# A hand-pipelined cross-attention and mixture kernel: the numerator a quarter later and ahead of kv on TensorE, delta and normalisation last in VectorE's quarter

## The chip, the core and the metric

The kernel runs on one core of a Trainium2 chip. The metric is the device time of one execution in microseconds. Before the change the median of three executions is 493.07 us (491.03 to 505.27). Float32 is used throughout, but for an exponential whose result is thrown away and for two operands of one product that are held as a high and a low part.

## What is computed

The input `x` has 8 x 512 rows of 2048 numbers, and so has the context. One attention layer and one mixture of low-rank experts (four experts, the best two of each row), each on a layer-normalised `x` and each added to `x`:

```python
def _L0_xattn_ref(q, k, v):              # q: layernorm(x); k = v: the context
    qh = q.transpose(0, 2, 1).reshape(B, N, H, dh)     # N = 2048, dh = 32
    ...
    qh = jax.nn.softmax(qh, axis=3)
    kh = jax.nn.softmax(kh, axis=1)
    kvs = jnp.einsum('bnhd,bnhe->bhde', kh, vh)
    out = jnp.einsum('bnhd,bhde->bnhe', qh, kvs)

def _L0_ffn_ref(x, router_w, A, B):      # x: layernorm(x + attention)
    logits = flat @ router_w.T
    topk_vals, topk_idx = jax.lax.top_k(logits, TOP_K)
    ...
    gates = jax.nn.softmax(sparse, axis=-1)
    mid = jnp.einsum('tf,erf->ter', flat, A)
    all_deltas = jnp.einsum('ter,eor->teo', mid, B) * LORA_SCALE
    delta = jnp.einsum('te,teo->to', gates, all_deltas)

x = x + _L0_xattn_ref(_layernorm(x), ctx, ctx)
x = x + _L0_ffn_ref(_layernorm(x), router_w, A, B)
```

(With 512 rows and 8 heads a head is 64 rows, so a tile of 128 rows holds two heads.)

## The kernel before, in words

The 4096 rows are 32 tiles of 128 rows, and each tile is cut into four groups of 512 columns. Nothing schedules the kernel but its text: every engine runs one loop over a step number `q` from -8 to 153, and in each step it does one group of each stage that is due. A step is called a quarter here. `tile_at(q, offset)` gives the tile `t` and the group `g` of a stage in quarter `q`: the stage does group `g` of tile `t` in quarter 4t + g + offset. Stages that come once in a tile ask for g = 0. The second layer works on pairs of tiles, with `pair_at` and `delta_at`. So a pair takes eight quarters, and within them the quarters are named here by q modulo 8 (0 to 7). Engines run ahead of each other as far as the semaphores let them.

The stages, with the engine, the name of the function, the line of the profile and the offset before the change:

- VectorE: `max_part` (L566, -8) the column maximum of the context; `bn_part` (L582, -4) the statistics of `x`, `ln1` (L589, L591) their end; `max_whole` (L575), once a tile, the maximum over the partitions of a turned tile; `kv_recip` (L611, offset 3), once a tile; `normalise` (offset 4) a reciprocal `rden` (L619) of the denominators in `num_ps` and the product `attnT` (L622); `add_delta` (L631) adds `delta_ps` to `y_sb`, which is the output; and, once a pair, a dozen small instructions of the router (`gate_...`), most of them in quarter 2; `mid_low` (L722) once a pair.
- TensorE: `delta` (L431, L432) makes `delta_ps`; `turn_max` and `spread_kmax` (L326, L333) once a tile; `kv` (L348, offset 0) 8 chunks of the product of keys and values; `project` (L384, offset 6) the router's and the experts' projection of `y_sb`; `fold_squares` (L398) once a tile, 32 matmuls, in quarters 2 and 6; `numerator` (L367, offset 4) makes `num_ps`; `turn_mid` (L417) once a pair. This is also their order in a quarter.
- GpSimd (POOL): `shift` (L275, -3) the context minus its maximum into `ek_sb`; `add_x` (L287, offset 4) adds `attnT` to `y_sb`; `root1` and `root2` (L295, L302 to L307).
- ScalarE (ACT): `keys` (L471) the exponential of `ek_sb` by half tiles, `queries` (L478) that of `x_sb`, in place, `square_x1` (L489) the squares of `y_sb`, and small copies (`spread_row` L464, `copy_kv` L499, `copy_squares` L507, `mid_high` L526).
- SyncE (SP): one queue that issues all transfers: `load_ctx` (L216), `load_x` (L220), `load_y` (L223) and `store` (L230), 1 MB each, each behind its wait.

There is one buffer each for `num_ps` and `delta_ps`: `numerator` of a group waits until `normalise` of the one before has read the bank (`attn_made`), and `delta` waits for the `add_delta` before it (`out_made`). `x_sb` has four tiles, and `load_x` of tile t waits for the last numerator of tile t - 4.

Of the kernel before, what the change touches and what calls it, by code (L numbers as in the profile page):

```python
# [44 lines left out]
def xattn_lora_moe_kernel(nc, x, xt, ctxt, wt, bt, consts, out):  # L45
# [11 lines left out]
    with ExitStack() as stack:  # L57
# [156 lines left out]
        def _(sp):  # L214
# [31 lines left out]
            for q in range(0, LAST + 3):  # L246
                p, i = delta_at(q - 1)
                if p is not None and i in (3, 7):
                    store(p, i // 4, 1 if p < NP - 1 else 4)
                t, g = tile_at(q, -12)  # L250
                if t is not None and t >= 4 and g == 0:
                    sp.wait_ge(kv_done, 4 * (t - 4) + 4)
                    load_ctx(t)
                t, g = tile_at(q, -8)
                if t is not None and t >= 3 and g == 0:
                    after(sp, num_done, 4 * (t - 4) + 4)
                    load_x(t)
                t, g = tile_at(q, -1)
                if t is not None and t >= 2 and g == 0:
                    if t >= 8:  # L260
                        old = (t - 8) // 2
                        sp.wait_ge(out_stored[old % 4], 32 * (old // 4 + 1))
                    load_y(t)
# [4 lines left out]
        def _(pool):  # L268
# [43 lines left out]
            for q in range(FIRST, LAST + 1):  # L312
                shift(*tile_at(q, -3))
                root2(q)
                add_x(*tile_at(q, 4))
                root1(q)

        @block.tensor
        def _(pe):
# [124 lines left out]
            for q in range(FIRST, LAST + 1):  # L444
# [4 lines left out]
                if q == 1:  # L449
                    sum_w()  # L450
                kv(*tile_at(q, 0))
                project(*tile_at(q, 6))
                fold_squares(q)
                numerator(*tile_at(q, 4))
# [3 lines left out]
        def _(act):  # L458
# [73 lines left out]
            for q in range(FIRST, LAST + 1):  # L532
                T, r = divmod(q, 4)
                if r == 0:
                    mid_high(q)
                    copy_kv(T - 1)
                    square_x1(T - 2, 1)
                    queries(T - 1, 1)
                if r == 1:
                    spread_row(T + 1)  # L540
                    keys(T, 1)
                if r == 2:
                    gate_exp(q)
                    square_x1(T - 1, 0)
                if r == 3:
                    copy_squares(T - 2)
                    keys(T + 1, 0)
                    queries(T, 0)
# [9 lines left out]
        def _(dve):  # L558
# [43 lines left out]
            def kv_recip(q):  # L602
                t, g = tile_at(q, 3)
# [121 lines left out]
            for q in range(FIRST, LAST + 1):  # L725
# [4 lines left out]
                mid_low(q)  # L730
# [4 lines left out]
                max_part(*tile_at(q, -8))  # L735
                if a is not None:
                    gate_centre(a)
                if b is not None:
                    gate_beats(b, 1)
                    gate_mask(b)  # L740
                ln1(q)
                add_delta(*delta_at(q))
                bn_part(*tile_at(q, -4))
# [4 lines left out]
                if not early:  # L748
                    max_whole(q)
                kv_recip(q)  # L750
                normalise(*tile_at(q, 4))
# [66 lines left out]
```

## Time and profile before

| | |
|---|---|
| median of three executions | 493.07 us (491.03 to 505.27) |
| the profiled execution | 493.56 us, of which its span (first to last instruction) 491.8 us |
| TensorE busy | 404.7 us (82%) |
| VectorE busy | 416.6 us (85%) |
| GpSimd busy | 358.9 us (73%) |
| ScalarE busy | 241.4 us (49%) |
| mean granted clock of TensorE | 0.944 |
| moved by DMA | 137.95 MB, mean 281 GB/s |

A timeline row gives the start and the length of an instruction (or of a run of alike ones) in us, and in brackets how long its engine had been idle before it and what ended that. Instructions of one engine overlap a little: on VectorE rows of 0.68 us start 0.60 us apart. A row of waits adds up such idle times by who waited for whom.

### The profile page before, as it was taken

Reading aid. Unit: us, or ns where it says so; the run is one execution under the profiler, and the core shown is the slowest. Engines: PE = TensorE matmul, PEld = TensorE weight load, DVE = VectorE, ACT = ScalarE, POOL = GpSimd, SP = SyncE. Lnnn points to the kernel's source line nnn. Section 1 sums busy time; section 2 is a strip of 40 time slices with the busy share of each in tenths; the row PEclk is TensorE's granted clock in tenths of the full one; section 3 lists DMA queues with packets and bytes.
Section 4 is the critical chain, followed back from the end, with each engine's and each line's share of the span. In section 5 each row is a group of like instructions: output and inputs, shape, how many; then the busy total and the mean of one; then the engine's idle time right before and its main releaser. Section 6 shows DMA issues by size and latency. Waiting matters only on the chain.

```text
span 491.8 us, 22601 instructions
## 1 busy us (share of the span) xinstructions
PE 404.7 (82%) x9960; PEld 346.6 (70%) x9960; DVE 416.6 (85%) x1109; ACT 241.4 (49%) x340; POOL 358.9 (73%) x341
## 2 busy tenths in 40 slices
PE   5477877979988898879888898979889887989764
PEld 5466766868777677768776777868677676878543
DVE  2598888989998999899987999989999998976652
ACT  1155556545555455555555356545655556564100
POOL 1369997878888787878877787887878786985200
PEclk9568999999999998999998999999999999999955
DMA  8987686587979797787977698887879795532243
GB/s 332 427 329 291 253 315 259 205 311 285 345 263 344 273 390 255 263 332 297 379 279 296 260 331 336 286 316 274 320 282 367 267 384 213 195 152 91 112 188 128
DMA packets 24689, 137.95 MB, mean 281 GB/s; under 512 B 2192, under 2 KB 4368, under 8 KB 12176
## 3 DMA queue, kind: packets, MB, share of 16 engines
q1 hardware_dynamic: 24592, 136.51, 73.5%
q8 instruction: 78, 1.28, 1.0%
q14 instruction: 19, 0.16, 0.1%
HBM read 102.95 MB, written 33.55 MB: 278 GB/s over the span
## 4 chain that ended last, share of the span: by engine, by line
PE 39%; DVE 35%; issue 16%; DMA 4%; POOL 3%; ACT 2%; SPq 1%; DVEq 0%; POOLq 0%
DVE y_sb L631 9%; PE num_ps L367 8%; DVE max_n L566 8%; PE kv_ps L348 7%; PE kv_ps L398 6%; PE delta_ps L431 6%; PE raw_ps L384 6%; DVE bn_parts L582 4%; DMA sq_a<-in_bt_dram 4%; PE delta_ps L432 3%; DVE rden L619 3%; DVE attnT L622 3%; POOL y_sb L287 2%; DVE rz L611 1%; DVE midT L722 1%
## 5 line engine op out<-in xcount | busy, mean ns | idle before, releaser
L287 POOL TENSOR_TENSOR y_sb<-attnT,y_sb 128x512 f32<-128x512 f32 x128 | 164.6, 1286 | 78.6 <-DVE attnT L622 77.3
L275 POOL TENSOR_TENSOR ek_sb<-ctx_sb,kmax_row 128x512 f32<-128x512 f32 x128 | 167.5, 1311 | 15.7 <-ACT kmax_row L464 15.7
L431 PE MATMUL delta_ps<-midT,b_hi 128*128 128x256 f32 x256 | 83.3, 346 | 38.2 <-DVE y_sb L631 37.0
L367 PE MATMUL num_ps<-kv_sb,x_sb 64*64 64x65 f32 x4096 | 94.5, 228 | 8.6 <-issue 7.5
L631 DVE TENSOR_TENSOR y_sb<-delta_ps,y_sb 128x512 f32<-128x512 f32 x128 | 87.5, 683 | 15.8 <-PE delta_ps L432 15.3
L348 PE MATMUL kv_ps<-ctx_sb,ek_sb 128*64 128x65 f32 x2048 | 94.0, 234 | 7.0 <-issue 4.2
L566 DVE TENSOR_REDUCE max_n<-ctx_sb 128x32 f32<-128x512 f32 x128 | 86.4, 677 | 10.8 <-DMA ctx_sb<-in_ctxt_dram 10.4
L622 DVE TENSOR_TENSOR attnT<-num_ps,rden 128x512 f32<-128x512 f32 x128 | 88.5, 691 | 4.6 <-DVE rden L619 0.2
L348 PEld LDWEIGHTS kv_ps<-ctx_sb,ek_sb 128*64 128x64 f32 x2048 | 75.1, 140 | 22.9 <-issue 8.8
L367 PEld LDWEIGHTS num_ps<-kv_sb,x_sb 64*64 64x64 f32 x4096 | 75.2, 137 | 22.6 <-issue 15.0
L384 PE MATMUL raw_ps<-w_sb,y_sb 128*64 128x69 f32 x2048 | 86.6, 225 | 4.4 <-issue 4.4
L431 PEld LDWEIGHTS delta_ps<-midT,b_hi 128*128 128x128 f32 x256 | 50.7, 198 | 54.7 <-DVE y_sb L631 30.3
L582 DVE BATCH_NORM_STATS2 bn_parts<-x_sb 128x6 f32<-128x512 f32 x128 | 87.5, 683 | 0.0
L478 ACT ACTIVATE x_sb<-x_sb,nbias,rstd 128x1024 f32<-128x1024 f32 x64 | 78.6, 1227 | 0.0
L384 PEld LDWEIGHTS raw_ps<-w_sb,y_sb 128*64 128x64 f32 x2048 | 74.5, 137 | 5.5 <-issue 5.1
L432 PE MATMUL delta_ps<-midT,b_lo 128*128 128x256 f32 x256 | 69.8, 293 | 2.3 <-issue 2.3
L471 ACT ACTIVATE ek_sb<-ek_sb 128x1024 f32<-128x1024 f32 x64 | 67.3, 1052 | 4.6 <-POOL ek_sb L275 3.6
L489 ACT ACTIVATE sq_a<-y_sb 128x1024 f32<-128x1024 f32 x32 | 33.9, 1059 | 69.9 <-POOL y_sb L287 69.9
L489 ACT ACTIVATE sq_b<-y_sb 128x1024 f32<-128x1024 f32 x32 | 33.9, 1058 | 61.7 <-POOL y_sb L287 61.7
L432 PEld LDWEIGHTS delta_ps<-midT,b_lo 128*128 128x128 f32 x256 | 51.8, 202 | 0.0
L619 DVE RECIPROCAL rden<-num_ps 128x8 f32<-128x8 f32 x128 | 25.9, 202 | 29.2 <-PE num_ps L367 28.2
L517 ACT ACTIVATE gexp<-below_max,rstd 128x4 f32<-128x4 f32 x32 | 7.8, 289 | 46.5 <-POOL rstd L307 41.9
(55 smaller groups left out, 324.7 us busy)
## 6 DMA issues: line engine op xcount, KB each, us to landing
ctx_sb<-in_ctxt_dram SPq DMA_DIRECT2D x32, 1040.0 KB, 5.6
x_sb<-in_x_dram SPq DMA_DIRECT2D x32, 1024.0 KB, 8.0
y_sb<-in_xt_dram SPq DMA_DIRECT2D x32, 1024.0 KB, 9.7
out_dram<-y_sb SPq DMA_DIRECT2D x30, 1024.0 KB, 5.9
out_dram<-y_sb SPq DMA_DIRECT2D x8, 256.0 KB, 2.1
sq_a<-in_bt_dram SPq DMA_DIRECT2D x1, 1024.0 KB, 18.5
w_sb<-in_wt_dram SPq DMA_DIRECT2D x1, 552.0 KB, 10.8
cst<-in_consts_dram SPq DMA_DIRECT2D x1, 145.0 KB, 2.3
```

The costliest lines, as they stand in the source:

```text
L275: pool.tensor_tensor(ek_sb[:, t % 2, chunks(g), :].rearrange("p (a b) c -> p a b c", b=2), ctx_sb[:, t % 4, 2 * g:2 * g + 2, 1:P + 1, :].r ...
L287: pool.tensor_tensor(y, attnT[:, g, :], y, ALU.add).then_inc(x1_made, 1)
L348: mm = pe.matmul(kv_ps[t % 2][d, h:h + DH + 1], ek_sb[:, t % 2, j, d], ctx_sb[:, t % 4, j // 2, v, j % 2], start=(j == 0), stop=(j == NCH ...
L367: mm = pe.matmul(num_ps[n, h, j * (DH + 1):(j + 1) * (DH + 1)], x_sb[d, t % 4, c * P + half * DH:c * P + (half + 1) * DH], kv_sb[d, t % 2, ...
L384: mm = pe.matmul(raw_ps[p % 2][c, odd, 0:NQ], y_sb[:, t % 8, j, c], w_sb[:, j, :], start=(odd == 0 and j == 0), stop=(j == NCH - 1), skip_ ...
L431: pe.matmul(to, b_hi[:, j * P:(j + 1) * P], midT[:, p % 2, :], start=True, stop=False)
L432: mm = pe.matmul(to, b_lo[:, j * P:(j + 1) * P], midT[:, p % 2, :], start=False, stop=True)
L478: act.activation(half, half, ACT.Exp, bias=nbias1[:, t % 4:t % 4 + 1], scale=rstd1[:, t % 4:t % 4 + 1]).then_inc(q_made, 1)
L566: dve.tensor_reduce(max_n[:, t % 2, c], ctx_sb[:, t % 4, :, 1 + g * 32:33 + g * 32, :].rearrange("p a c b -> p c a b"), AX.XY, ALU.max).th ...
L582: dve.bn_stats(bn_parts[:, t % 4, g, :], x_sb[:, t % 4, cols(g)]).then_inc(bn_parts_made, 1)
L622: dve.tensor_tensor(attnT[:, g, :].rearrange("p (k b d) -> p b k d", b=2, d=DH), heads[:, :, :, 0:DH], rden[:].unsqueeze(3).to_broadcast([ ...
L631: dve.tensor_tensor(y, delta_ps[:].rearrange("p (j t c) -> p t j c", j=2, t=2), y, ALU.add).then_inc(out_made, 1)
```

## The change

The numerator moves from offset 4 to offset 5 and, within TensorE's quarter, from behind `project` and `fold_squares` to the place ahead of `kv`. What follows it moves a quarter with it: `normalise` and `add_x` to offset 5, `project` to offset 7. `kv_recip` goes from offset 3 to 4 and to the second place in VectorE's quarter; `bn_part`, `ln1` and `max_whole` come ahead of `mid_low` and `add_delta`, so that `add_delta` and `normalise` are the last large instructions of a VectorE quarter. On ScalarE both `square_x1` halves come later (the first in the next tile's quarter 0, the second behind `keys` in quarter 1), and `queries(T, 0)` goes from quarter 3 to quarter 2. On SyncE `load_x` moves by one quarter. Nothing is added or removed: each engine runs the same instructions with the same operands.

```diff
@@ sync
-                t, g = tile_at(q, -8)
+                t, g = tile_at(q, -7)
                 if t is not None and t >= 3 and g == 0:
                     after(sp, num_done, 4 * (t - 4) + 4)
                     load_x(t)
@@ gpsimd
-                add_x(*tile_at(q, 4))
+                add_x(*tile_at(q, 5))
@@ tensor
+                numerator(*tile_at(q, 5))
                 kv(*tile_at(q, 0))
-                project(*tile_at(q, 6))
+                project(*tile_at(q, 7))
                 fold_squares(q)
-                numerator(*tile_at(q, 4))
                 turn_mid(q)
@@ scalar
                 if r == 0:
                     mid_high(q)
+                    square_x1(T - 2, 0)
                     copy_kv(T - 1)
-                    square_x1(T - 2, 1)
                     queries(T - 1, 1)
                 if r == 1:
                     spread_row(T + 1)
                     keys(T, 1)
+                    square_x1(T - 2, 1)
                 if r == 2:
                     gate_exp(q)
-                    square_x1(T - 1, 0)
+                    queries(T, 0)
                 if r == 3:
                     copy_squares(T - 2)
                     keys(T + 1, 0)
-                    queries(T, 0)
@@ vector, kv_recip
-                t, g = tile_at(q, 3)
+                t, g = tile_at(q, 4)
@@ vector, the loop
-                mid_low(q)
                 if b is not None:
                     gate_beats(b, 0)
                 if c is not None:
                     gate_mid(c)
                 max_part(*tile_at(q, -8))
+                kv_recip(q)
                 if a is not None:
                     gate_centre(a)
                 if b is not None:
                     gate_beats(b, 1)
                     gate_mask(b)
+                bn_part(*tile_at(q, -4))
                 ln1(q)
+                if not early:
+                    max_whole(q)
+                mid_low(q)
                 add_delta(*delta_at(q))
-                bn_part(*tile_at(q, -4))
                 if a is not None:
                     gate_logits(a)
                 if b is not None:
                     gate_rank(b)
-                if not early:
-                    max_whole(q)
-                kv_recip(q)
-                normalise(*tile_at(q, 4))
+                normalise(*tile_at(q, 5))
```

On TensorE, in the middle of the program, quarters 1 and 2 of a pair stood like this before (`delta_ps` is the mixture's product, `kv_ps` the attention's, `raw_ps` the projection, `num_ps` the numerator):

```order
L431 MATMUL delta_ps<-midT,b_hi 128x256
L432 MATMUL delta_ps<-midT,b_lo 128x256
L333 MATMUL turn_ps<-cst,kmax 128x128
L348 MATMUL kv_ps1<-ctx_sb,ek_sb 64x65 x8
L384 MATMUL raw_ps1<-w_sb,y_sb 64x69 x8
L367 MATMUL num_ps<-kv_sb,x_sb 64x65 x16
L431 MATMUL delta_ps<-midT,b_hi 128x256
L432 MATMUL delta_ps<-midT,b_lo 128x256
```

and stand like this now:

```order
L431 MATMUL delta_ps<-midT,b_hi 128x256
L432 MATMUL delta_ps<-midT,b_lo 128x256
L333 MATMUL turn_ps<-cst,kmax 128x128
L367 MATMUL num_ps<-kv_sb,x_sb 64x65 x16
L348 MATMUL kv_ps1<-ctx_sb,ek_sb 64x65 x8
L384 MATMUL raw_ps1<-w_sb,y_sb 64x69 x8
L431 MATMUL delta_ps<-midT,b_hi 128x256
L432 MATMUL delta_ps<-midT,b_lo 128x256
```

The numerator has gone from the end of the quarter to the place behind the delta.

On VectorE, quarters 3 and 4 of a pair stood like this before (`rz` is `kv_recip`, `midT` is `mid_low`):

```order
L566 TENSOR_REDUCE max_n<-ctx_sb 128x32
L631 TENSOR_TENSOR y_sb<-delta_ps,y_sb 128x2x256
L582 BN_STATS bn_parts<-x_sb 128x6
L611 RECIPROCAL rz<-kv_ps0 64x1 x2
L619 RECIPROCAL rden<-num_ps 128x8
L622 TENSOR_TENSOR attnT<-num_ps,rden 128x2x4x64
L722 TENSOR_TENSOR midT<-raw_ps1,midT 64x256
L566 TENSOR_REDUCE max_n<-ctx_sb 128x32
L589 BN_AGGR bn_out<-bn_parts 128x2
L591 TENSOR_SCALAR var1e<-bn_out 128x1
L631 TENSOR_TENSOR y_sb<-delta_ps,y_sb 128x2x256
L582 BN_STATS bn_parts<-x_sb 128x6
```

and stand like this now, but for the first two:

```order
L631 TENSOR_TENSOR y_sb<-delta_ps,y_sb 128x2x256
L619 RECIPROCAL rden<-num_ps 128x8
L622 TENSOR_TENSOR attnT<-num_ps,rden 128x2x4x64
L566 TENSOR_REDUCE max_n<-ctx_sb 128x32
L611 RECIPROCAL rz<-kv_ps0 64x1 x2
L582 BN_STATS bn_parts<-x_sb 128x6
L589 BN_AGGR bn_out<-bn_parts 128x2
L591 TENSOR_SCALAR var1e<-bn_out 128x1
L575 TENSOR_REDUCE kmax<-turn_ps 128x1
L722 TENSOR_TENSOR midT<-raw_ps1,midT 64x256
L631 TENSOR_TENSOR y_sb<-delta_ps,y_sb 128x2x256
L619 RECIPROCAL rden<-num_ps 128x8
```

Between the start of a quarter and `add_delta` there is now `bn_stats` too, and `rz` and the other small work of the tile have moved ahead of both readers of TensorE's results.

On the SyncE queue a tile's four transfers now stand like this (before, `x_sb` stood ahead of `out_dram`):

```order
L216 DMA ctx_sb<-in_ctxt_dram 128x2080
L230 DMA out_dram<-y_sb 128x2x1024
L220 DMA x_sb<-in_x_dram 128x2048
L223 DMA y_sb<-in_xt_dram 128x2048
```

The load of `x` is now behind a store that waits for `add_delta` of quarter 4 or 0.

## Rows read from the trace of the kernel before

**Rows 1.** Windows of four stretches: busy us by engine, granted clock, DMA share, GB/s.

```profile
core 0: us, PE busy (x) PEld busy (x) DVE busy (x) ACT busy (x) POOL busy (x), PEclk, DMA share, GB/s
34.00:84.00 50.00, 39.10 (x1128) 33.47 (x1130) 41.49 (x110) 28.00 (x38) 44.26 (x39) 0.93 0.74 283
84.00:425.00 341.00, 295.02 (x7699) 253.32 (x7702) 316.21 (x850) 183.50 (x260) 275.77 (x260) 0.99 0.80 299
425.00:458.00 33.00, 30.62 (x829) 26.35 (x824) 26.01 (x82) 17.87 (x26) 24.18 (x25) 1.00 0.35 130
458.00:492.00 34.00, 19.80 (x133) 15.06 (x132) 14.85 (x35) 2.21 (x5) 2.37 (x4) 0.64 0.42 155
```

**Rows 2.** Waits, 84 to 425 us: total us, times, longest.

```profile
POOL y_sb L287 <- DVE attnT L622: 61.9, 61, 2.7
...
PE delta_ps L431 <- DVE y_sb L631: 26.9, 30, 1.5
...
DVE rden L619 <- PE num_ps L367: 15.2, 23, 3.2
```

**Rows 3.** Waits, 34 to 84 us.

```profile
DVE rden L619 <- PE num_ps L367: 7.2, 7, 2.0
...
PE kv_ps L348 <- ACT ek_sb L471: 2.6, 3, 0.9
```

**Rows 4.** Timeline of VectorE, one quarter 6 (columns as told above).

```profile
364.30 0.68 DVE L566 TENSOR_REDUCE max_n<-ctx_sb 128x32 f32<-128x512 f32 x1
364.89 0.68 DVE L631 TENSOR_TENSOR y_sb<-delta_ps,y_sb 128x512 f32<-128x512 f32 x1
365.49 0.69 DVE L582 BATCH_NORM_STATS2 bn_parts<-x_sb 128x6 f32<-128x512 f32 x1
366.45 0.21 DVE L619 RECIPROCAL rden<-num_ps 128x8 f32<-128x8 f32 x1 [0.28 <-PE num_ps L367]
366.70 0.69 DVE L622 TENSOR_TENSOR attnT<-num_ps,rden 128x512 f32<-128x512 f32 x1
```

**Rows 5.** Timeline of TensorE, the same quarter 6, with the delta ahead of it.

```profile
362.88 0.39 PE L431 MATMUL delta_ps<-midT,b_hi 128*128 128x256 f32 x1
...
363.55 0.71 PE L348 MATMUL kv_ps<-ctx_sb,ek_sb 128*64 128x65 f32 x16
364.10 0.66 PE L384 MATMUL raw_ps<-w_sb,y_sb 128*64 128x69 f32 x16
364.68 0.65 PE L398 MATMUL kv_ps<-sq_a,cst 128*32 128x128 f32 x16
...
365.69 0.70 PE L367 MATMUL num_ps<-kv_sb,x_sb 64*64 64x65 f32 x32
```

**Rows 6.** Timeline of TensorE, a gap with no releaser, and near the end.

```profile
265.85 0.94 PE L384 MATMUL raw_ps<-w_sb,y_sb 128*64 128x69 f32 x13 [1.89 <-issue]
...
462.49 0.39 PE L431 MATMUL delta_ps<-midT,b_hi 128*128 128x256 f32 x1
```

**Rows 7.** Timeline of VectorE behind that gap, and the last normalise.

```profile
269.73 0.21 DVE L619 RECIPROCAL rden<-num_ps 128x8 f32<-128x8 f32 x1 [3.15 <-PE num_ps L367]
...
457.29 0.69 DVE L622 TENSOR_TENSOR attnT<-num_ps,rden 128x512 f32<-128x512 f32 x1
```

**Rows 8.** Timeline of ScalarE in the first stretch.

```profile
68.97 1.06 ACT L489 ACTIVATE sq_b<-y_sb 128x1024 f32<-128x1024 f32 x1 [2.07 <-POOL y_sb L287]
...
71.22 1.04 ACT L471 ACTIVATE ek_sb<-ek_sb 128x1024 f32<-128x1024 f32 x1
```

**Rows 9.** Timeline of GpSimd, the first two add_x.

```profile
35.78 2.19 POOL L287 TENSOR_TENSOR y_sb<-attnT,y_sb 128x512 f32<-128x512 f32 x1 [3.90 <-DVE attnT L622]
...
39.70 1.26 POOL L287 TENSOR_TENSOR y_sb<-attnT,y_sb 128x512 f32<-128x512 f32 x1
```

**Rows 10.** The page's DMA issues: KB each, median us to landing.

```profile
x_sb<-in_x_dram SPq DMA_DIRECT2D x32, 1024.0 KB, 8.0
```

**Rows 11.** The page's DMA queues: packets, MB, share of 16 engines.

```profile
q8 instruction: 78, 1.28, 1.0%
```
## The prediction

> **What bounds the kernel now.** I read the windows by stage first, then the waits of each stage, then two timelines side by side. Four stretches differ [rows 1]. From 84 to 425 us, where all stages run, VectorE is busy for 316.2 of 341 us (93%), TensorE for 87%, GpSimd for 81%. From 34 to 84 us there is no delta yet, and GpSimd is the fullest (44.3 of 50 us). From 425 to 458 us VectorE has run out of `max_part` and `bn_part`, and TensorE is the fullest (30.6 of 33 us). Behind 458 us deltas alone run, two engines in turn.
>
> In the long stretch VectorE waits for one thing: the numerator, 23 times, 15.2 us in all. TensorE in turn waits 26.9 us for `add_delta` [rows 2]. So the two are tied in a ring with little room. The rest of VectorE's idle time there (341 - 316.2 - 15.2 = 9.6 us) is short waits between its own dependent instructions, which the change keeps.
>
> The timelines show the room. On VectorE a large instruction takes a step of 0.60 us (364.30, 364.89, 365.49), the reciprocal and the product together 0.86 us [rows 4], so a plain quarter takes 3 x 0.60 + 0.86 = 2.66 us. On TensorE the steps from start to start are delta 0.67, kv 0.55, project 0.58, fold 1.01 and numerator 0.63 us (the last from its length less what the next overlaps) [rows 5]: 2.43 us in a plain quarter, 3.44 with the fold. Light quarters follow each other (5, 6, 7), and in them TensorE has about as much to do as VectorE.
>
> Let T be the start of a VectorE quarter. Before, `delta` of the next quarter can start when `add_delta` ends, at T + 0.60 + 0.68 = 1.28; delta, kv, project and numerator end at 3.71; the next `normalise` wants it at 2.66 + 1.80 = 4.46. Room: 0.75 us; with the fold 4.72, which is 0.26 us late. The trace has 0.28 us there [rows 4]. So this way of counting holds, and I use it for the new order.
>
> **The change, part by part.** No instruction is added or removed, so busy times stay; only waits can change.
>
> *The ring in the long stretch.* Now numerator(q) starts when `normalise` of q - 1 ends, at about T, and ends at 0.63; kv ends at 1.18, project at 1.76, the fold at 2.77. Delta of the next quarter also needs `add_delta`, which ends at 1.20 + 0.68 = 1.88; so delta ends at 2.55, or 3.44 with the fold. It is wanted at 2.66 + 1.20 = 3.86. The next numerator starts at 2.72 (behind `normalise`) or 3.44 and ends at 3.35 or 4.07; it is wanted at 4.46. The room is the smaller difference: 1.11 us in a plain quarter (0.75 before), 0.39 with the fold (-0.26 before). It grows by 0.36 to 0.65 us. (`kv_recip` made quarter 7 longer than 2.66 us before and no longer does; the counts of the new order are without it.)
>
> Most of the 15.2 us isn't the fold's 0.3 us but what follows a gap on TensorE that no releaser explains: one of 1.89 us [rows 6], after which matmuls ran at half the speed for a while and VectorE waited 3.15 us [rows 7]. More room cuts each such wait by 0.36 to 0.65 us and doesn't remove it. Cutting each of the 23 waits [rows 2] by 0.45 us or by all of it takes off 8.7 us; by 0.65 us, some 10.5. I take 9.5 us, with 7 and 15.2 (all of it) as bounds.
>
> On those gaps the Trainium skill has a rule ("Runtime: NRT & Kernel Launch", Instruction fetch mechanics): instructions are streamed in blocks of 16 KB through a queue of their own, and the crossing of a block is mostly hidden. This trace has such a queue, 78 packets and 1.28 MB [rows 11], but it doesn't say what the gaps are. If fetching is hidden, as the rule has it, the gaps are something the order might remove, and the gain would be the full 15.2 us: the first rival below. I count with the gaps as the rows have them, which stay.
>
> *The first stretch.* Here VectorE waits 7.2 us for the numerator, and TensorE 2.6 us for the keys [rows 3]. The chain is on ScalarE: `square_x1` waited 2.07 us for `add_x`, and `queries`, `spread_row` and `keys` stood behind it until 71.22 us [rows 8]; kv waited for the keys, and the numerator stood behind kv. Both links go: `keys(T, 1)` is now ahead of the square, and the numerator ahead of kv. GpSimd then runs at its own pace, about 2.5 us a quarter (two instructions of some 1.25 us), of which 50 - 44.3 = 5.7 us were idle, 3.9 of that at the very start [rows 1, 9]. At the start quarter 4 loses its `normalise` (0.86 us), and GpSimd an `add_x` (1.26 us) out of this stretch, whose second stood at 39.70 [rows 9]. I take 4 us for both together, with 0 (gaps eat it) and 6 as bounds.
>
> *From 425 to 458 us.* TensorE's work is the sum there and stays: nothing.
>
> *The end.* The numerator of the last group comes a quarter later, so quarter 132 gets one. Before, from the end of the last `normalise` (457.98) to the delta behind the last fold (462.49) there are 4.5 us [rows 6, 7]. Now that quarter is longer by `normalise` and by the numerator (about 2.0 us in all), and from its end `add_x` (1.3), the squares (1.06), the fold (1.01) give 3.5 us: 5.5 against 4.5. It costs 1 us; bounds 0 and 2.
>
> *The other moves cost nothing as long as their cover stands.* `queries(T, 0)` in quarter 2 is wanted in quarter 5. `square_x1(T - 2, 1)` in quarter 1 is ready some 2.4 us into it and the fold comes 1.8 us into the next. `mid_low` stands 1.9 us into quarter 4, wanted in 5. `shift` behind a late `add_x` reaches `keys` 2 us before kv. ScalarE has 46% to spare [rows 1]. Were the cover of one gone, a wait of about 1 us per tile, 30 us, would follow.
>
> *`load_x` behind the store.* The store waits for `add_delta` of quarter 4 or 0, whose end is 0.9 us before the next quarter. In the light half the load is then issued about 0.2 us before quarter 5 and `bn_part` wants it 1.0 us into quarter 8: 3 x 2.66 + 0.2 + 1.0 = 9.2 us. The median landing before is 8.0 us [rows 10], with one other transfer ahead of it; now there is also one ahead. Covered by 1.2 us, at nothing.
>
> The sum, on the profiled execution: 493.6 - 9.5 - 4 + 1 = 481.1 us. The median of three was 0.5 us below that execution; I say 481.
>
> **The rivals.**
> - *All waits for the numerator go* (0.14). The ring has more room everywhere, and if the gaps shrink with it, the full 15.2 us go and 4 more: 493.6 - 15.2 - 4 + 1 = 475 us. Against it: gaps of up to 1.9 us are longer than 1.1 us of room.
> - *The gain stays small* (0.17). TensorE's light stretch is full; a longer semaphore path than I count, or gaps that come while it catches up, leave the waits as they are, and the head of the program is held by its loads: 493.6 - 2 + 1 = 492, in a range of 486 to 495.
> - *`x` lands late* (0.06), the other sign. The store and the two loads now leave together. If landing takes 11 us instead of 8.0, `bn_part` waits 1.8 us in each tile: 28 x 1.8 = 50 us if each is late, 25 if every second: 506 us and more. It decides from a landing of 9.2 us on. Against it: DMA engines are 80% busy in this stretch [rows 1], so 20% is free, and the loads have the same sizes.
> - *Another cover is gone* (0.05), on ScalarE or GpSimd: 488 to 510.
>
> **How the numbers follow.** My forecast has 0.58, with 476 to 486 us for its own range. Faster by over 2% (about what a measurement of this kernel tells from no change) means below 483.2 us: three quarters of the forecast's chance and the first rival's, 0.44 + 0.14 = 0.58. Slower: 0.06 and half of the last, 0.09. Same: the rest, 0.33. The range must leave out no more than 0.2: from 473 to 490 us it leaves out the late cases (0.11), part of the small gain and little below.
>
> **What would show it.** Right: in the long stretch VectorE's waits for the numerator fall from 15.2 to about 6 us and TensorE's quarter is no longer than VectorE's; the fold's quarters show none; kv waits for no keys in the first stretch; no waits of VectorE for `x`. Wrong: waits of `bn_part` for a DMA; waits of `add_delta` for TensorE in the place of those for the numerator; a later first `add_x`; or gaps of TensorE that are more or longer than now.

## The result, and the profile of the changed kernel

The changed kernel is slower: a median of 518.21 us (514.55 to 526.65, four executions) against 492.65 us (491.03 to 505.27) of the kernel before, a ratio of 1.049 with an interval of 1.0426 to 1.0553. I had predicted 481 us, in a range of 473 to 490: the sign was wrong. The profiled execution of the changed kernel (526.65 us, about 8 us above its median) is one of its slow ones, and so are those of e1 (521.52), e3 (523.61) and e10 (506.50) below, so gaps and waits are read from them, but the size of a loss from the ratios, which leave such executions out.

Its page, busy times and then the shares of the chain of work that ended last:

```profile
span 524.9 us, 22601 instructions
...
PE 422.6 (81%) x9960; PEld 366.0 (70%) x9960; DVE 419.0 (80%) x1109; ACT 242.2 (46%) x340; POOL 357.1 (68%) x341
...
PE 43%; DVE 31%; issue 18%; DMA 3%; POOL 2%; SPq 1%; ACT 1%; DVEq 0%; POOLq 0%
```

Every engine runs the same number of instructions. VectorE is busy 2.4 us longer than before, TensorE 17.9 us longer: its matmuls ran at a lower clock. The windows of the same stretches as in [rows 1] (the last one is longer here):

```profile
34.00:84.00 50.00, 42.72 (x1157) 37.15 (x1159) 42.77 (x112) 29.09 (x40) 43.94 (x41) 0.84 0.70 266
84.00:425.00 341.00, 280.11 (x6949) 242.80 (x6948) 288.26 (x769) 167.92 (x237) 250.21 (x236) 0.93 0.77 279
```

In the long stretch the clock is 0.93 instead of 0.99, and no engine is as full as before; VectorE fell from 316.2 to 288.3 us of 341. What it waits for there answers to [rows 2]:

```profile
DVE y_sb L631 <- PE delta_ps L432: 38.4, 13, 5.8
...
PE kv_ps L398 <- issue: 14.0, 5, 3.4
PE raw_ps L384 <- issue: 13.8, 6, 4.0
...
PE kv_ps L348 <- issue: 12.0, 5, 4.0
...
PE num_ps L367 <- issue: 7.3, 6, 1.8
...
DVE rden L619 <- PE num_ps L367: 4.0, 8, 1.6
```

The wait for the numerator did go, from 15.2 to 4.0 us. `add_delta` now waits for TensorE instead, 13 times, 38.4 us in all, up to 5.8 us each. And TensorE itself stood without a releaser ("issue": it waited for nothing that the profile shows) for about 47 us in these four rows.

Where the time came in can be read off one small instruction that both kernels have 16 times, in the same quarter of each pair (the first of the router, `negmean`, L638): its first and last starts are

```profile
L638 DVE TENSOR_SCALAR negmean<-raw_ps x16: 147/148/151, 70.6 to 465.4; 128x2 f32<-128x2 f32 x16
```

in the kernel before and

```profile
L638 DVE TENSOR_SCALAR negmean<-raw_ps x16: 148/149/152, 69.6 to 498.5; 128x2 f32<-128x2 f32 x16
```

in the changed one. Up to the first it is 1.0 us shorter, between first and last 34.1 us longer (428.9 against 394.8), and behind the last the same (26.4 and 26.4). So the whole loss, 33.1 us of span between these two executions (25.6 us between the medians), is in the part where tiles follow each other.

**One event.** Here is TensorE in one of the long ones (start, length, what ran; in brackets the idle time before):

```profile
112.01 0.63 PE L348 MATMUL kv_ps<-ctx_sb,ek_sb 128*64 128x65 f32 x13
116.61 0.37 PE L348 MATMUL kv_ps<-ctx_sb,ek_sb 128*64 128x65 f32 x2 [3.97 <-issue]
...
117.94 1.08 PE L398 MATMUL kv_ps<-sq_a,cst 128*32 128x128 f32 x16
...
120.96 1.03 PE L367 MATMUL num_ps<-kv_sb,x_sb 64*64 64x65 f32 x32
```

It stopped in the middle of `kv`, after 13 of 16 matmuls, for 3.97 us, and waited for nothing that the profile shows. Afterwards half a fold took 1.08 us (0.65 in [rows 5]) and the numerator 1.03 (0.70). VectorE lost more than the gap:

```profile
114.58 0.68 DVE L582 BATCH_NORM_STATS2 bn_parts<-x_sb 128x6 f32<-128x512 f32 x1
121.07 0.69 DVE L631 TENSOR_TENSOR y_sb<-delta_ps,y_sb 128x512 f32<-128x512 f32 x1 [5.80 <-PE delta_ps L432]
```

The windows show clock and transfers in the same time (columns as in [rows 1]):

```profile
112.00:114.00 2.00, 0.64 (x20) 0.49 (x13) 1.97 (x6) 0.72 (x1) 2.00 (x2) 1.00 0.97 363
114.00:116.00 2.00, 0.00 (x0) 0.00 (x0) 1.26 (x3) 0.00 (x0) 2.00 (x3) 0.72 1.02 418
116.00:118.00 2.00, 1.39 (x23) 1.26 (x27) 0.00 (x0) 0.00 (x0) 0.77 (x1) 0.50 0.68 279
118.00:120.00 2.00, 2.00 (x34) 1.50 (x34) 0.00 (x0) 0.06 (x1) 0.00 (x0) 0.50 0.02 8
```

While TensorE stands, the DMA engines are full (0.97 and 1.02). It starts again as they run empty. The granted clock is 0.50 then, 1.2 GHz instead of 2.4; the trace has it there from 114.9 to 121.7 us. What filled the DMA engines is on the SyncE queue:

```profile
107.90 0.40 SPq L230 DMA_DIRECT2D out_dram<-y_sb  x1
108.34 0.47 SPq L220 DMA_DIRECT2D x_sb<-in_x_dram  x1
112.98 0.33 SPq L223 DMA_DIRECT2D y_sb<-in_xt_dram  x1
...
125.88 0.40 SPq L230 DMA_DIRECT2D out_dram<-y_sb  x1
126.32 0.47 SPq L220 DMA_DIRECT2D x_sb<-in_x_dram  x1
126.83 0.96 SPq L223 DMA_DIRECT2D y_sb<-in_xt_dram  x1
```

Store and `x` leave 0.4 us apart, 1 MB each, and in every second tile `y` 0.5 us behind them. The kernel before issued `x` some 3 us ahead of the store (and 1.1 us behind the context):

```profile
202.01 0.33 SPq L220 DMA_DIRECT2D x_sb<-in_x_dram  x1
205.12 0.39 SPq L230 DMA_DIRECT2D out_dram<-y_sb  x1
```

**What a gap is.** I counted TensorE's instructions in the trace in their order (matmuls, weight loads and the others, 20,126 in all). Each gap of 0.5 us or more without a releaser behind 84 us, in both kernels, begins at an instruction whose number is 193 plus a multiple of 256 (where that is a weight load or a semaphore, the matmul is one or two further on): in the changed kernel 4033 (the one above), 5313, 6593, 7873, 9665, and so on. The queue "instruction" of [rows 11] moves 1.28 MB in 78 packets, 16 KB each; 20,126 / 78 is 258. So a packet looks like a block of 256 instructions of 64 bytes, and a gap like a wait for the next packet. The Trainium skill ("Runtime: NRT & Kernel Launch", Instruction fetch mechanics) has blocks of 16 KB or 256 instructions; that part the count bears out. Its "mostly hidden" does not hold here. The kernel before has 13 such gaps, 16.5 us in all, the longest 2.27 us; the changed one 25, 52.9 us in all, nine of 2.5 us or more, the longest 3.99.

The trace has the packets themselves, and they bear this out. For the event above, the DMA queues of the changed kernel from 106 to 114 us, and then from 114 to 116 us (packets, MB, share of 16 engines), are

```profile
q1 hardware_dynamic: 453, 2.41, 84.8%
...
q1 hardware_dynamic: 115, 0.82, 99.2%
q8 instruction: 1, 0.02, 2.8%
```

TensorE began its block at 106.2 us. No packet of instructions came for 8.0 us; the next ran from 114.2 to 115.1 us, and TensorE went on at 116.6. I take the packets in order, one for each following block. Then each of the 38 gaps of the two kernels ends 2.2 to 2.6 us after the start of such a packet, and no block behind 84 us starts less than some 2.2 us after the start of its packet. So the gaps are waits for packets of instructions. What made a packet late is the question of the experiments.

### The profile page after: what moved, and what is told of

It reads as the page before. It is cut to its first block, busy times and chain, and to the rows that moved or that the text cites. A ratio compares the mean times of both kernels' runs of the same rounds, so it can differ in the third digit from the quotient of the medians.

```text
span 524.9 us, 22601 instructions
## 1 busy us (share of the span) xinstructions
PE 422.6 (81%) x9960; PEld 366.0 (70%) x9960; DVE 419.0 (80%) x1109; ACT 242.2 (46%) x340; POOL 357.1 (68%) x341
## 3 DMA queue, kind: packets, MB, share of 16 engines
q8 instruction: 78, 1.28, 1.0%
## 4 chain that ended last, share of the span: by engine, by line
PE 43%; DVE 31%; issue 18%; DMA 3%; POOL 2%; SPq 1%; ACT 1%; DVEq 0%; POOLq 0%
PE num_ps L367 10%; DVE y_sb L631 8%; PE kv_ps L348 8%; PE delta_ps L431 7%; PE raw_ps L384 7%; PE kv_ps L398 6%; DVE max_n L566 6%; DVE bn_parts L582 5%; PE delta_ps L432 4%; DMA sq_a<-in_bt_dram 3%; DVE attnT L622 3%; DVE rden L619 2%; POOL y_sb L287 1%; DVE rz L611 1%; DVE midT L722 1%
## 5 line engine op out<-in xcount | busy, mean ns | idle before, releaser
L348 PE MATMUL kv_ps<-ctx_sb,ek_sb 128*64 128x65 f32 x2048 | 97.8, 240 | 13.7 <-issue 13.7
L367 PE MATMUL num_ps<-kv_sb,x_sb 64*64 64x65 f32 x4096 | 97.3, 234 | 13.2 <-issue 8.4
L384 PE MATMUL raw_ps<-w_sb,y_sb 128*64 128x69 f32 x2048 | 91.8, 231 | 16.9 <-issue 16.9
L431 PE MATMUL delta_ps<-midT,b_hi 128*128 128x256 f32 x256 | 87.0, 359 | 21.8 <-DVE y_sb L631 20.2
L367 PEld LDWEIGHTS num_ps<-kv_sb,x_sb 64*64 64x64 f32 x4096 | 79.1, 143 | 31.6 <-issue 20.2
L348 PEld LDWEIGHTS kv_ps<-ctx_sb,ek_sb 128*64 128x64 f32 x2048 | 78.3, 145 | 23.6 <-issue 14.3
L384 PEld LDWEIGHTS raw_ps<-w_sb,y_sb 128*64 128x64 f32 x2048 | 79.1, 143 | 18.7 <-issue 18.0
L432 PE MATMUL delta_ps<-midT,b_lo 128*128 128x256 f32 x256 | 72.7, 302 | 0.0
L507 ACT ACTIVATE sq_sum<-kv_ps 128x128 f32<-128x128 f32 x32 | 8.7, 272 | 82.4 <-PE kv_ps L398 82.3
L398 PE MATMUL kv_ps<-sq_a,cst 128*32 128x128 f32 x512 | 25.0, 307 | 11.6 <-issue 11.4
```

Of the source, the lines that this page charges most:

```text
L348: mm = pe.matmul(kv_ps[t % 2][d, h:h + DH + 1], ek_sb[:, t % 2, j, d], ctx_sb[:, t % 4, j // 2, v, j % 2], start=(j == 0), stop=(j == NCH ...
L367: mm = pe.matmul(num_ps[n, h, j * (DH + 1):(j + 1) * (DH + 1)], x_sb[d, t % 4, c * P + half * DH:c * P + (half + 1) * DH], kv_sb[d, t % 2, ...
L384: mm = pe.matmul(raw_ps[p % 2][c, odd, 0:NQ], y_sb[:, t % 8, j, c], w_sb[:, j, :], start=(odd == 0 and j == 0), stop=(j == NCH - 1), skip_ ...
L431: pe.matmul(to, b_hi[:, j * P:(j + 1) * P], midT[:, p % 2, :], start=True, stop=False)
L432: mm = pe.matmul(to, b_lo[:, j * P:(j + 1) * P], midT[:, p % 2, :], start=False, stop=True)
```

## The experiments

Theory A, in all expectations: transfers that now leave together make TensorE's next instructions late; take that away and the order of the change gains what was predicted. Theory B: the new order itself costs the time (its `add_delta` waits), whatever the transfers do. Each ratio is to executions of the kernel before that were timed beside the run. Gaps are again those of 0.5 us or more behind 84 us.

**Undo and do the one line on SyncE.** `e1_x_ahead` is the changed kernel with

```diff
-                t, g = tile_at(q, -7)
+                t, g = tile_at(q, -8)
```

for `load_x`, and `e2_before_x_behind` the kernel before with the opposite.

> The changed kernel with one part undone: load_x stands ahead of the store again (offset -8). Theory A (the store, the load of x and often the load of y now leave together; the blocks of instructions for TensorE, which come by DMA too, arrive late behind them, and TensorE stands still for 3 to 4 us once a pair): the gaps fall back to 1 to 2 us and the time to 480 to 488 us. Theory B (the new order of the stages on TensorE and VectorE is what costs, and the gaps are longer by chance or for another reason): 512 to 520 us, as the changed kernel.

> The kernel before with one part of the change alone: load_x behind the store (offset -7). Theory A: the same gaps of 3 to 4 us as in the changed kernel, once a pair, and with the slow clock behind them 508 to 520 us. Theory B: 490 to 496 us, as before, since x has time to land.

Measured: e1 513.64 us, ratio 1.0394 (1.028 to 1.0509); e2 510.60 us, 1.0355 (1.027 to 1.0441). Moving `load_x` behind the store makes the kernel before 3.5% slower, with nothing else changed: 21 gaps, 38.3 us. Its VectorE waits 30.7 us for the numerator, twice the 15.2 of [rows 2]. That is most of the loss, and theory A. But the line put back in e1 regained little (28 gaps, 51.3 us), and its time lies in the range of theory B. Its SyncE rows tell one reason:

```profile
225.48 0.33 SPq L220 DMA_DIRECT2D x_sb<-in_x_dram  x1
225.86 1.11 SPq L230 DMA_DIRECT2D out_dram<-y_sb  x1
```

`load_x` stands ahead of the store again, but leaves 0.4 us ahead of it in some tiles: it waits for the last numerator of tile t - 4, which the change has put a quarter later. From 84 to 425 us SyncE waits there for 51.3 us in e1, and for 30.8 us in the kernel before:

```profile
SPq L220 <- PE num_ps L367: 51.3, 22, 5.3
```

The position in the queue was undone, the time was not. So the order of the stages has a part in when transfers leave, and e1 alone doesn't tell that part from a cost of the order itself.

**Hold `y` apart.** `e3_y_paced` is the changed kernel with a wait ahead of `load_y`, `e4_both` has this and the line of e1:

```diff
+                    sp.wait_ge(kv_done, 4 * t - 1)
                     load_y(t)
```

> The changed kernel, with load_x still behind the store, but load_y held back until the third kv group of the tile before (kv_done at 4t - 1), so that at most the store and x leave together. Theory A: gaps of 1 to 2 us, 485 to 500 us. Theory B: 512 to 520 us.

> The changed kernel with load_x ahead of the store and load_y held back as well: the four transfers of a tile leave about evenly spaced. Theory A: the smallest gaps, 475 to 486 us, no slower than with load_x ahead alone. Theory B: 512 to 520 us.

Measured: e3 518.37 us, 1.0475 (1.0344 to 1.0605), 22 gaps of 43.9 us; e4 511.0 us, 1.0266 (1.0115 to 1.0417), 31 gaps of 46.6 us. Both missed theory A's numbers; e3 lies in theory B's range, e4 1 us below it. Three transfers within 2 us of each other are gone in both, and the gaps are not.

**Less to transfer.** `e5_before_light` and `e6_after_light` leave out part of the work: from tile 4 on only a quarter of the context's columns is loaded, from tile 8 on a quarter of `y`, and stores write a quarter. Every instruction of the four other engines is as it was.

```diff
-                sp.dma_start(y_sb[:, t % 8, :, :], xt[t]).then_inc(y_landed[t % 8], 16)
+                c = slice(0, 16 if t < 8 else 4)
+                sp.dma_start(y_sb[:, t % 8, c, :], xt[t][:, c]).then_inc(y_landed[t % 8], 16)
```

> The kernel before with less traffic: a store sends a quarter of its columns, and the loads of the context from tile 4 on and of y from tile 8 on bring a quarter; x is loaded whole (a tile moves 1.8 MB and not 4.1), so the output is not the reference's. Theory A (TensorE's unexplained gaps are blocks of instructions that arrive late behind the bulk transfers): the gaps of over 0.5 us vanish, and the time falls by the 15 us that VectorE waits for the numerator or most of it, to 478 to 487 us. Theory B (the gaps have to do with the order of the stages, not with transfers): gaps and time stay, 490 to 496 us.

> The changed kernel with the same lighter traffic. Theory A: without late blocks the ring of TensorE and VectorE has the room that the prediction counted, and the time is 470 to 482 us, below that of the kernel before with the same traffic by 3 to 12 us (some of its waits being gone already). Theory B: it stays above the kernel before with the same traffic, by 10 to 25 us.

Measured: e5 485.85 us, 0.9865 (0.978 to 0.995), no gap at all, as theory A has it, and

```profile
DVE rden L621 <- PE num_ps L369: 6.1, 15, 0.8
```

in the long stretch, where it was 15.2 us in [rows 2]. So some 9 of the 15.2 us went with the gaps. e6 took 499.13 us, 1.0167 (1.008 to 1.0254): the changed kernel still had 14 gaps, 23.1 us, and was 13 us slower than e5: theory A's number was missed, theory B's was met. It issues three transfers within 2 us as the changed kernel does.

**Even spacing.** `e7_after_even` is the changed kernel with both loads behind a wait on `kv`'s progress, `e8_before_even` the kernel before with the same two, and `e9_after_even_light` is e7 with the smaller transfers of e6 (the same part left out):

```diff
-                t, g = tile_at(q, -7)
+                t, g = tile_at(q, -6)
...
+                    sp.wait_ge(kv_done, 4 * t - 6)
                     load_x(t)
...
+                    sp.wait_ge(kv_done, 4 * t - 1)
                     load_y(t)
```

> The changed kernel with its four transfers of a tile held apart, at least two thirds of a quarter between any two: store when its add_delta is done, x a quarter later (gate: kv_done at 4t - 6, which is group 4t - 7), y a quarter after that (kv_done at 4t - 1), the context when its buffer is free. All bytes are moved. Theory A: no more than one transfer lies ahead of a block; gaps of 1 us at most, 474 to 490 us. Theory B: 508 to 520 us.

> The kernel before with the same gates on x and y. Theory A: its gaps shrink as well, 480 to 492 us, and the changed kernel with even transfers is faster than this by 3 to 12 us. Theory B: 490 to 496 us, gaps as before.

> The changed kernel with even transfers and with the lighter traffic (1.8 MB a tile; the output is not the reference's). With the light traffic alone the changed kernel still took 499 us and had 14 gaps in its long stretch, the kernel before 486 and none. Theory A (the late blocks come from transfers that leave together when a block is asked for, and the new order is worth what was predicted once they are gone): no gap over 0.5 us, and 472 to 481 us, below the kernel before with light traffic. Theory B (the new order also has a cost or a lack of its own): 484 us or more, with VectorE waiting for TensorE outside gaps.

SyncE in e7 now issues never less than 2.4 us apart, mostly some 3 us:

```profile
200.51 0.33 SPq L216 DMA_DIRECT2D ctx_sb<-in_ctxt_dram  x1
203.72 0.40 SPq L230 DMA_DIRECT2D out_dram<-y_sb  x1
206.73 0.33 SPq L220 DMA_DIRECT2D x_sb<-in_x_dram  x1
210.87 0.33 SPq L223 DMA_DIRECT2D y_sb<-in_xt_dram  x1
```

Measured: e7 490.57 us, 0.9963 (0.9925 to 1.0001), 19 gaps of 23.7 us, none of 2.5 us. Against 1.049 of the changed kernel that is some 26 us less, with every byte still moved and no engine's order touched but SyncE's: the spacing of the transfers is the loss. Its gaps (up to 2.16 us) are more than theory A's 1 us, though, and its time is just above the range. e8 gave 488.83 us, 0.9931 (0.989 to 0.9972), 13 gaps of 10.8 us: in theory A's range, but e7 is not faster than it, as that theory had it. e9 gave 481.01 us, 0.9723 (0.9676 to 0.977), one gap, 1.2 us, at the upper end of theory A's range; 481 us, the time predicted, comes only with well under the traffic of the real kernel, and with a part of the work left out.

So theory B, that the order itself loses the time whatever the transfers do, has fallen: with its transfers held apart the order loses nothing. But at even spacing the order gains nothing either (e7 is no faster than e8).

Here are the issue times of all of these together, the three with lighter traffic last. The counts are those of SyncE's issues from 84 to 425 us; gaps are those of 0.5 us or more behind 84 us. Both are from one profiled execution of each kernel.

| | issues under 0.6 us apart | three within 3.5 us | gaps, sum in us | ratio |
|---|---|---|---|---|
| before | 12 | 4 | 13, 16.5 | 1 |
| changed | 31 | 14 | 25, 52.9 | 1.049 |
| e1_x_ahead | 22 | 28 | 28, 51.3 | 1.0394 |
| e2_before_x_behind | 28 | 12 | 21, 38.3 | 1.0355 |
| e3_y_paced | 22 | 3 | 22, 43.9 | 1.0475 |
| e4_both | 6 | 20 | 31, 46.6 | 1.0266 |
| e7_after_even | 0 | 0 | 19, 23.7 | 0.9963 |
| e8_before_even | 0 | 0 | 13, 10.8 | 0.9931 |
| e5_before_light | 13 | 0 | 0 | 0.9865 |
| e6_after_light | 31 | 26 | 14, 23.1 | 1.0167 |
| e9_after_even_light | 0 | 0 | 1, 1.2 | 0.9723 |

Of the eight with full traffic, the five with 20 or more issues in bunches of either kind have 38 us of gaps or more, the two with none 24 or less, and the kernel before, with few bunches, 16.5. Less traffic lowers the gaps at like bunching (e5 against before, e6 against changed, e9 against e7). Neither column alone orders the rows, so which bunches hurt is open.

**Smaller pieces.** `e10_after_halves` (on e7) and `e11_before_halves` (on e8) issue each load as two of 0.5 MB, the second behind a wait on `attn_made`:

```diff
+            def load_x(t, q=None):
+                for i in halves(q):
+                    c = slice(i * H2, (i + 1) * H2)
+                    sp.dma_start(x_sb[:, t % 4, c], x_rows[t * P:(t + 1) * P, c]).then_inc(x_landed[t % 4], 16)
```

> The changed kernel with even transfers, each cut in two halves of 0.5 MB, the second held until the normalise of the same quarter (attn_made), about half a quarter later. All bytes are moved. Theory A: fewer bytes lie ahead of a block, gaps sum to less than half of those with even whole transfers (23.7 us from 84 us on), and 478 to 487 us. Theory B: as with even whole transfers, 488 to 493 us.

> The kernel before with even transfers in the same halves. Theory A: its gaps shrink too (10.8 us with whole transfers), 482 to 488 us, and the changed order with halves is 2 to 8 us faster than this. Theory B: 486 to 490 us and no slower than the changed order with halves.

Measured: e10 505.25 us, 1.0141 (1.0056 to 1.0226), 26 gaps of 41.0 us; e11 496.21 us, 1.0024 (0.9973 to 1.0074), 13 gaps of 14.5 us. Both missed both theories: these kernels were slower than e7 and e8. But they are no runs of small pieces held apart. In e10 the wait between the halves had mostly been met already, and from 84 to 425 us the second left 0.65 us behind the first in the median. In e11 the halves are 2.7 us apart, but 35 times a second half left less than 0.6 us ahead of the next load, which never happened in e8.

**Fewer instructions, the same transfers.** If gaps are late packets of instructions, fewer instructions must thin them out with the transfers left as they are. `e12_after_fewer` is the changed kernel, `e15_before_fewer` the kernel before, `e13_before_even_fewer` and `e14_after_even_fewer` are e8 and e7, each with one matmul where `kv` had one for each head and `project` one for each half:

```diff
-                    for h in range(2):
-                        d = slice(h * DH, (h + 1) * DH)
-                        v = slice(h * (DH + 1), (h + 1) * (DH + 1))
-                        mm = pe.matmul(kv_ps[t % 2][d, h:h + DH + 1], ek_sb[:, t % 2, j, d],
-                                       ctx_sb[:, t % 4, j // 2, v, j % 2],
-                                       start=(j == 0), stop=(j == NCH - 1), skip_group_check=True)
+                    mm = pe.matmul(kv_ps[t % 2][:, 0:VW], ek_sb[:, t % 2, j, :],
+                                   ctx_sb[:, t % 4, j // 2, :, j % 2],
+                                   start=(j == 0), stop=(j == NCH - 1), skip_group_check=True)
```

> The changed kernel, transfers and order untouched, with fewer TensorE instructions for the same work: kv takes both heads in one matmul of 130 columns (the two cross blocks are not read), project takes a tile's 128 columns in one matmul and not in two halves. That is 16 instructions less in each kv and project of the trace's 32 matmuls and 32 weight loads, so about 1,000 and not 1,245 a pair; TensorE's busy time may change by some per cent either way. Theory A (a block of 256 instructions that comes late ends TensorE's work): fewer blocks are asked for per pair (3.9 and not 4.9) and each lasts longer, so the gaps sum to 30 us or less (52.9 now) and the time is 485 to 505 us. Theory C (the gaps come from the grouping of the transfers in another way than through blocks of instructions, such as a stall of TensorE's operands): as many gaps of the same size per pair, 510 to 520 us.

> The kernel before with even transfers and with the fewer TensorE instructions: theory A has almost no gaps left (10.8 us now) and 476 to 486 us, a version below both kernels; theory C has 486 to 491 us.

> The changed kernel with even transfers and with the fewer TensorE instructions: theory A has gaps below 8 us (23.7 now), and 472 to 483 us, so that the new order shows what it is worth with all bytes moved, 1 to 2% below the order before; theory C has 488 to 493 us.

> The kernel before with the fewer TensorE instructions alone: theory A has gaps of 5 us or less (16.5 now), 480 to 488 us; theory C has 490 to 496 us.

Measured: e12 503.72 us, 1.0248 (1.013 to 1.0367); e13 516.66, 1.0506 (1.0415 to 1.0596); e14 503.17, 1.0231 (1.0143 to 1.032); e15 516.36, 1.0494 (1.0405 to 1.0584). The time of e12 is in its range; the three others missed, since the long matmuls are slower than I took them for. The gaps are what these runs were for: 1 of 0.84 us in e12, none in the three others. e12's page has fewer packets of instructions and almost no "issue" in its chain:

```profile
q8 instruction: 62, 1.02, 0.8%
...
PE 89%; DVE 5%; DMA 3%; issue 1%; SPq 1%; ACT 0%
```

e12 still issues three transfers within 3.5 us 23 times (changed: 14), so the bunching is not less. Its TensorE has 16,030 instructions instead of 20,126, 989 in a pair of tiles instead of 1,245. A pair takes 27.2 us in e12 (407.8 us between the first and the last `negmean`, over 15 pairs) and 26.3 us in the kernel before, so 256 instructions last some 7.0 us instead of 5.4. Gaps thus need both: bulk transfers under way (more gaps where these leave together, but 19 and 13 also in e7 and e8, where they don't), and a TensorE that gets through a block before the next one has come.

Between e12 and e15, where no gaps disturb, the new order can be read by itself: 503.7 against 516.4 us, 12.7 us less; e14 against e13, the same pair with even transfers, gives 13.5 us. TensorE is the full engine in both e12 and e15 (busy for 340.2 and 330.8 of 341 us), and VectorE's waits in the long stretch are, in e12 and then in e15,

```profile
DVE y_sb L629 <- PE delta_ps L427: 18.9, 12, 2.6
```

```profile
DVE rden L617 <- PE num_ps L364: 26.0, 48, 1.2
```

Where TensorE bounds, the new order is worth 12.7 / 516.4 = 2.5%.

**Only `project` merged.** `e16_after_even_proj` is e7 with the second merge alone, `e17_after_even_proj_heavy` the same in quarters 0 to 4 of each pair only:

```diff
+                    parts = 1 if (4 * t + g + 7) % 8 in (0, 1, 2, 3, 4) else 2
+                    for part in range(parts):
+                        c = slice(part * P // parts, (part + 1) * P // parts)
```

> The changed kernel with even transfers and only project in one matmul per chunk (kv stays split by heads). By the lengths in the run with both merged a project takes 0.84 us and not 0.58, and a pair has some 1,117 TensorE instructions. Theory A: the gaps shrink from 23.7 us to 5 to 12, but in the light quarters 5 to 7 TensorE now has 0.26 us more in each and VectorE waits about 1 us a pair more, so 484 to 492 us. Theory C (no gap theory): 494 to 500 us.

> The same with project merged only in quarters 0 to 4 of a pair, where VectorE has more to do than TensorE, and split in 5 to 7: 1,165 instructions a pair. Theory A: the longer matmuls are covered, gaps of 8 to 16 us, and 480 to 488 us, the fastest with all bytes moved and below both kernels. If the gaps don't shrink or the longer projects aren't covered: 490 us or more.

Measured: e16 489.71 us, 0.9937 (0.9903 to 0.9971), 4 gaps of 4.4 us, the time in theory A's range; e17 488.73 us, 0.9935 (0.9902 to 0.9968), 11 gaps of 10.8 us, just above the expected range. With e8 these are the best that compute everything: 0.6 to 0.7% below the kernel before, three versions that can't be told apart. In both the gaps begin at instruction 193 + 256k again, though a pair now has other numbers of instructions. And e16 needs 26.2 us from one pair to the next, as e7 does, so its fewer gaps (4.4 us against 23.7) come with the fewer instructions and not with a slower pair.

## Why the prediction was wrong, step by step

- **`load_x` behind the store, "at nothing": the step that failed.** I asked only whether `x` would land in time. It did: the median landing rose from 8.0 us [rows 10] to 8.4, and VectorE never waited for it, so the rival "x lands late" didn't happen either. I didn't ask who else waits on the DMA engines. TensorE's instructions do. With that line alone the kernel before loses 3.5% (e2), against 4.9% for the whole change. And there was a second way to the same bunches that my count hadn't: the numerator a quarter later holds `load_x` back as well, so that without the moved line the new order still loses 3.9% (e1). With the transfers held apart both losses are gone (e7).
- **The gaps "stay" as the rows have them: failed with it.** I had 13 gaps and the queue of [rows 11] in front of me, and left open what they were. Their sum went from 16.5 to 52.9 us, 36 us more, against 33.1 us of span in the same executions. The first rival (gaps shrink with the order) had the wrong sign too. My list of what would show me wrong named gaps "more or longer than now", and waits of `add_delta` in place of those for the numerator: both came.
- **The ring, −9.5 us: mis-sized.** The counting of room held in kind: the waits for the numerator fell from 15.2 to 4.0 us. But most of the 15.2 us went with the gaps (6.1 left in e5 without any). In e9 VectorE waits 5.4 us for the delta and 0.3 for the numerator, 5.7 in all against 6.1 in e5:

```profile
DVE y_sb L635 <- PE delta_ps L436: 5.4, 11, 0.7
```

  Without gaps, then, these waits are the same where VectorE is the fuller engine. Between the first and last `negmean` it is 385.9 us in e9 and 384.0 in e5. The room taken from one reader of TensorE's results was given to the other. So these profiles put the term at about 0, but the one of e5 is the fastest of its executions (481.19 us, median 485.85): by the ratios (0.9723 and 0.9865, intervals that nearly touch) e9 gains 1.4% on e5, some 7 us, of which the first stretch explains 3. A few us of the term may thus exist, not the 9.5. With heavy matmuls (e12 against e15) the change was worth 12.7 us in all, as much as was predicted, but there TensorE is the full engine.
- **The first stretch, −4 us:** the kind was right. The second `add_x` of [rows 9] at 39.70 has its answer in the first at 37.51, 2.2 us earlier:

```profile
37.51 1.28 POOL L287 TENSOR_TENSOR y_sb<-attnT,y_sb 128x512 f32<-128x512 f32 x1 [1.02 <-DVE attnT L622]
```

  Up to the first `negmean` the changed kernel kept 1.0 us of it, with its gaps; e9 has 3.2 us against e5 (65.7 and 68.9).
- **The end, +1 us:** from the end of the `normalise` of quarter 131 to the delta behind the last fold it is 5.98 us against 4.5 before, +1.5 us; predicted +1. The time behind the last `negmean` is the same, 26.4 us in both, so by that measure it did not reach the end. (Its three terms 1.3, 1.06 and 1.01 add up to 3.4, not 3.5.)
- **The other moves at nothing:** no cover of `queries` or the keys shows up among the waits. `mid_low` is one that I passed over too lightly. I counted 1.20 us ahead of `add_delta`; in quarter 4 `rz`, the end of the statistics, `kmax` and `mid_low` stand there too. In one such quarter of e9 it starts 2.8 us behind `max_part`. In e9 the weights of the delta of quarter 5 wait for `mid_low`,

```profile
PEld delta_ps L435 <- DVE midT L726: 21.2, 12, 1.8
```

  its matmuls for the `add_delta` behind it, and behind such an idle time `kv` takes 1.13 us instead of 0.71 in e9 (the granted clock is 0.50 from 321.5 to 324.9 us):

```profile
320.16 0.36 PE L435 MATMUL delta_ps<-midT,b_hi 128*128 128x256 f32 x1 [1.68 <-DVE y_sb L635]
...
321.68 1.13 PE L352 MATMUL kv_ps<-ctx_sb,ek_sb 128*64 128x65 f32 x16
```

  That may be part of why e9 is not faster; it was not tried apart.

**What stays open.** How a packet of instructions comes to wait behind transfers of another queue was not seen, only that it comes later. From 84 to 425 us, from the start of one block on TensorE to the packet of the next, it took 2.33 us in the mean before (longest 5.16), 2.78 us after (longest 8.02) and 1.06 us in e5 with the light traffic, beside the 5.4 us that a block lasts. Nor do I know why e3, with threes gone, kept 43.9 us of gaps, and whether smaller pieces that are really held apart would help. And e7 still has more gaps than e8 (23.7 against 10.8 us) with the same gates, though its issues are no closer together (2.4 us at least, 1.5 in e8).

## What to carry to other kernels

Before a transfer is moved in a queue, read when it will leave and beside which others, not only whether it lands in time: an engine's own instructions come over the same DMA engines, and two megabytes that left together, with a third 5 us behind, kept a full TensorE standing for 4 us here and left it at 1.2 GHz behind that. An idle time that no releaser explains deserves a count of the instructions ahead of it: here all of them had the same number modulo 256, and what thinned them out was to space the transfers (e7), to move fewer bytes (e5) or to have fewer instructions (e12). And a buffer's release that moves later takes the load behind it along, though its line stands where it stood.

## What the hardware showed that I had not expected

- The gaps at instruction 193 + 256k, up to 3.99 us, each ending 2.2 to 2.6 us after the start of a packet of instructions, and the clock of 0.50 behind each of the nine of 2.5 us or more (6.8 us of it behind the one shown).
- Two matmuls with 64 columns of weights cost less than one with 128 here. From start to start `kv` took 0.55 us in 16 matmuls of 65 moving columns [rows 5] and takes 1.03 in 8 of 130; `project` 0.58 in 16 and 0.81 in 8, all of 69:

```profile
200.96 1.19 PE L345 MATMUL kv_ps<-ctx_sb,ek_sb 128*128 128x130 f32 x8
201.99 1.00 PE L379 MATMUL raw_ps<-w_sb,y_sb 128*128 128x69 f32 x8
202.80 0.36 PE L426 MATMUL delta_ps<-midT,b_hi 128*128 128x256 f32 x1
```

- Loads in halves used more of the DMA engines for no more bytes a second: in the long stretch a share of 0.85 at 293 GB/s in e10 and 0.83 at 305 in e7, 0.89 at 303 in e11 and 0.82 at 305 in e8.
